# Scaling attention probabilities on GpSimd: a tensor-scalar multiply replaced by a product of two tensors

## The reference, cut to what matters

```python
scores = einsum('bhqd,bhkd->bhqk', Q, K_rep) / 8
scores = scores + polarity_bias + (1 - gtp) * NEG
attn   = softmax(scores, axis=-1)
out    = einsum('bhqk,bhkd->bhqd', attn, V_rep)
```

## Time and profile before

| what | value |
|---|---|
| median of 3 runs | 4389.04 us (4388.15 to 4399.78) |
| span of the profiled execution, first to last instruction | 4385.1 us |
| PE busy | 3923.2 us, 89% |
| DVE busy | 3009.0 us, 69% |
| ACT busy | 2583.3 us, 59% |
| POOL busy | 2416.3 us, 55% |
| mean granted TensorE clock | 0.966 of full speed |
| line L1420 (the scaling), 768 instructions on POOL | 927.1 us busy |

### The profile page before, as it was taken

The page is one execution under the profiler, slowest core; times in us unless marked ns, Lnnn a source line. Parts: engine busy times, 40 slices in busy tenths (PEclk is TensorE's granted clock), DMA queues, the critical chain, the costliest instruction groups (busy, mean ns, idle before and its releaser), DMA issues. The chain is left out here.

```text
span 4385.1 us, 105712 instructions
## 1 busy us (share of the span) xinstructions
PE 3923.2 (89%) x37596; PEld 2574.9 (59%) x37596; DVE 3009.0 (69%) x8821; ACT 2583.3 (59%) x6209; POOL 2416.3 (55%) x3854
## 2 busy tenths in 40 slices
PE   3999999999999999999999999829599999999999
PEld 1565555555556655555555566526366666666666
DVE  4676676676666766766666766562387877788786
ACT  2656556556566565565565665502277777777776
POOL 3657566566475565665664755525455545555452
PEclk7999999999999999999999999959799999999999
DMA  4323334233243233342432432123332433324231
GB/s 126 75 77 84 75 76 92 66 95 85 62 99 73 78 82 77 78 93 65 96 79 68 97 75 77 49 94 60 54 64 45 61 58 54 59 49 70 45 54 26
DMA packets 168566, 317.06 MB, mean 72 GB/s; under 512 B 21680, under 2 KB 112112, under 8 KB 162928
## 3 DMA queue, kind: packets, MB, share of 16 engines
q1 hardware_dynamic: 162928, 300.88, 32.0%
q0 software_dynamic: 3968, 5.25, 0.7%
q10 hardware_dynamic: 1152, 4.19, 0.3%
HBM read 126.66 MB, written 32.59 MB: 36 GB/s over the span
## 5 line engine op out<-in xcount | busy, mean ns | idle before, releaser
L1420 POOL TENSOR_SCALAR l_prob_wo<-l_prob_wo,l_recip_g 128x384 f32<-128x384 f32 (+3 forms) x768 | 927.1, 1219 | 259.5 <-DVE l_recip_g L980 257.6
L1871 DVE TENSOR_REDUCE l_neg_max<-l_bank 128x1 f32<-128x512 f32 x1024 | 680.3, 684 | 260.5 <-PE l_bank L1710 259.9
L1997 ACT ACTIVATE l_pts<-l_bank 128x512 f32<-128x512 f32 x1024 | 593.3, 597 | 296.8 <-PE l_bank L1725 288.1
L1248 ACT ACTIVATE l_prob_wo<-l_prob_wo,l_neg_max_g 128x128 f32<-128x128 f32 (+3 forms) x1024 | 571.0, 559 | 297.9 <-DVE l_neg_max_g L974 291.4
L961 DVE CUSTOM_DVE_ANT_0 l_bank<-l_bank,l_mask 128x128 f32<-128x128 f32 (+3 forms) x1024 | 501.0, 500 | 319.8 <-PE l_bank L648 311.9
L974 DVE CUSTOM_DVE_ANT_0 l_prob_wo<-l_bank,l_bias 128x128 f32<-128x128 f32 (+3 forms) x1024 | 476.1, 483 | 342.5 <-PE l_bank L699 319.6
L1240 ACT ACTIVATE l_pts<-l_bank 128x128 f32<-128x128 f32 (+3 forms) x1024 | 439.3, 437 | 443.2 <-PE l_bank L666 426.8
L710 PE MATMUL l_bank<-ident,l_prob_wo 128*128 128x128 f32 x2560 | 426.5, 283 | 84.0 <-POOL l_prob_wo L1420 38.1
L710 PEld LDWEIGHTS l_bank<-ident,l_prob_wo 128*128 128x128 f32 x2560 | 289.1, 141 | 317.0 <-issue 178.6
L1710 PE MATMUL l_bank<-next_ks,l_qs 96*128 96x512 bf16 x1024 | 393.5, 385 | 46.2 <-DVE l_neg_max L1871 23.1
L1725 PEld LDWEIGHTS l_bank<-l_qs,next_ks 128*128 128x128 bf16 x4096 | 303.5, 97 | 181.1 <-ACT l_pts L1997 30.6
(11 more groups left out here) (262 smaller groups left out, 8081.2 us busy)
## 6 DMA issues: line engine op xcount, KB each, us to landing
l_bias<-bias SPq DMA_DIRECT2D x128, 512.0 KB, 4.4
l_qs<-l_parts SPq DMA_DIRECT2D x192, 128.0 KB
l_qs<-l_qs SPq DMA_DIRECT2D x96, 256.0 KB
l_x<-in_x SPq DMA_DIRECT2D x32, 512.0 KB, 4.7
l_kT<-l_bias SPq DMA_DIRECT2D x128, 128.0 KB, 3.2
l_qT<-l_arena SPq DMA_DIRECT2D x128, 128.0 KB, 3.0
l_qT<-l_bias SPq DMA_DIRECT2D x128, 128.0 KB, 3.0
l_prob_wo<-in_Wo SPq DMA_DIRECT2D x16, 1024.0 KB, 4.8
```

Of the source, the lines that this page charges most:

```text
L1248: nc.scalar.activation(prob[qt][:, i, :], prob[qt][:, i, :], ACT.Exp, bias=neg_max_g[:, k:k + 1], scale=-1.0, accum_out=sums_g[:, k:k + 1] ...
L1420: nc.gpsimd.tensor_scalar(prob[qt][:, i, :], prob[qt][:, i, :], recip_g[:, k:k + 1], None, ALU.mult).then_inc(s.g_scaled, 1)
L1871: nc.vector.tensor_reduce(neg_max[:, n % (2 * UNITS):n % (2 * UNITS) + 1], S[n % SB][:, :], AX.X, ALU.max, negate=True).then_inc(s.max_rea ...
L1997: nc.scalar.activation(pts[:, q % 2, u % H, :, :], TB[u % 2][:, :].rearrange("p (j q) -> p j q", j=NT), ACT.Exp, scale=DS ** -0.5).then_in ...
```

## The change

`scale` multiplied a row by a per-partition scalar: an instruction with one tensor operand and a pointer to a column of 128 numbers. It now multiplies two tensors: the row, and that same column read at step 0, so that each of the row's (qt + 1) * 128 elements meets the same number. Output, semaphores, waits, and the place in POOL's list are the same, and no other instruction of any engine is changed or moved.

```diff
                     k = 2 * p + i
                     pool.wait_ge(s.g_recip, BEATS * b + p + 1)
-                    nc.gpsimd.tensor_scalar(prob[qt][:, i, :], prob[qt][:, i, :], recip_g[:, k:k + 1], None, ALU.mult).then_inc(s.g_scaled, 1)
+                    v = prob[qt][:, i, :]
+                    nc.gpsimd.tensor_tensor(v, v, recip_g[:, k:k + 1].to_broadcast([P, (qt + 1) * P]), ALU.mult).then_inc(s.g_scaled, 1)
```

## The result

The changed kernel took **4402.73 us** (median of 20 runs, 4389.03 to 4414.11), the kernel before 4395.52 (20 runs, 4388.15 to 4404.54): a ratio of 1.0023, 95% interval 1.0015 to 1.0031. That is 7 us slower, inside the 0.3% that was counted as no change, and 35 us above the forecast.

A forecast was written before the change was run, and what follows sets the result against it. PE bounds the kernel, busy 89% of the span; PE waits shortened by 0.69 + 0.41 + 0.23 = 1.33 us in each of 16 sequences save 21 us, giving 4368 us against 4389.04. The 8-in-10 range was 4350 to 4403 us.

The forecast's parts named there:

- the first rival: Slower: POOL's product shuts out DVE's own scaling L984 until it ends, delaying copy and PE; 4415 us, chance 0.17.
- L1081's lead of 0.13 us: Evidence against shut-out: a 256-wide DVE operation starting 0.13 us ahead of a POOL product kept its 0.35 us.
- first sign of being wrong: L984's mean at 256 wide at 0.7 us or more, PE's waits for L993 growing as much as POOL's fall.
- The rival's price: At 256-wide beats, L984 shut out would end at 0.84 instead of 0.35 us, making PE 0.49 us later; 47 us altogether.
- The three places: PE's waits on POOL at 512-wide, 384-wide and a sequence's last row: gains 0.69, 0.41 and 0.23 us, 1.33 a sequence.
- the fourth place: PE's transpose of a 128-wide beat: wait put down to POOL but really for DVE's 512-wide copy; counted as nothing.
- the bound: All PE idle time ending with a scaled row from POOL, about all a faster POOL can give: 38.1 us.
- six places in a sequence: 256-wide beats where shut-out would delay PE by 0.49 us each, over 16 sequences: 47 us.
- The count that the price went by: Eight times in a sequence a 256-wide L984 starts about 0.06 us before POOL's L1420.
- the second rival: No change: other engines close behind give the gain back at the second and third place; 11 us remain, 4378 us, chance 0.22.
- the 17 forecast: PE's waits on POOL fall from 38.1 to about 17 us, what is left being the second and fourth place.
- the change does what it says: Opposing rival: step 0 is read dearly, new instruction no shorter than 1572 ns at 512; 4389 us or more, chance 0.04.

The follow-up runs named there:

- E5: The change plus a one-column POOL memset to an unused tile before each 128- and 256-wide product: 4365.05 us, 0.993 of the kernel before.
- E4: The change, with POOL's 128- and 256-wide products also waiting until DVE's scaling L984 is done: 4363.5 us, 0.993 of the kernel before.
- E2: The change with the new instruction at 384 and 512 wide only, the old one at 128 and 256: 4360.58 us, 0.9931 of the kernel before.
- E9: The change itself, run again beside E7's kernel on one chip: 4404.52 us, 1.002 of the kernel before.
- E10: E7's kernel, run again beside the change on one chip: 4379.15 us, 0.9974 of the kernel before.
- E1: The change with all rows scaled on POOL by the new instruction, DVE's scaling L984 removed: 4362.82 us, 0.9928 of the kernel before.
- E7: The change with DVE's 128-wide scaling moved to POOL, DVE keeping only the 256-wide one: 4379.55 us, 0.9959 of the kernel before.
- E8: The kernel before with all rows scaled on POOL by the old instruction, none on DVE: 4411.89 us, 1.0035 of the kernel before.

## Why the prediction was wrong

**The step that failed** is the weighing of the first rival: "Against it: DVE's start is the earlier one". I took a lead of 0.06 us, read off the start stamps beside the old instruction, and L1081's lead of 0.13 us, which was enough, and gave the rival 0.17. The leads in the change are 0.04 and 0.05 us, and they lose every time; 0.08 us wins every time (E5). L1081's row lay on the far side of that limit and said nothing of the near side. The prediction itself noted that the lead would be smaller; between two outcomes with no row in between, a chance near one half was due. What the runs showed is the rival's mechanism: L984 at 256 wide took 0.81 us in 113 of 128 cases, and PE's waits for L993 rose from 28.8 to 75.5 us, more than those for POOL fell. That is the prediction's own first sign of being wrong.

**What was right.** The instruction: 1044, 828, 621 and 424 ns against estimates of 1049, 835, 622 and 409, and POOL's busy time fell by 331 us (322). The rule of the Trainium skill, "GPSIMD Engine Reference", section "Engine selection" (against VectorE, one-input operations at about line rate, two-input ones about half as fast), isn't borne out where the scalar comes from a column: 1572 ns for the one, 1044 for the product. The rival's price: L984 took 0.81 (0.84), ending 0.15 us behind POOL (0.16). The three places: in the second sequence of the change the waits of 0.69 and 0.23 are gone, and that of 1.10 has shrunk by 0.46 (0.41 forecast):

```profile
426.98 0.55 PE L710 MATMUL l_bank<-ident,l_prob_wo 128*128 128x128 f32 x3 [0.64 <-POOL l_prob_wo L1421]
```

Right, too, was that POOL's wait at the fourth place isn't POOL's: it is 0.44 us in E4, as before.

**What the change alone is worth.** With L984 kept out of the way in E4, it is -26 us in front of L710 and -30 in the median; 21 were forecast, 38 as the bound. Some 5 us of the rest lie in a row that wasn't read: waits for ACT's copies (15.7 to 10.4). The shutting-out then costs 88.2 - 56.5 = 32 us in front of L710, where 0.49 us at six places in a sequence made 47: at the place shown above PE lost 0.42 (0.86 for 0.44), and 32 us over 16 sequences is 2.0 us, or nearly five such places. The count that the price went by was misread as well: L984 at 256 wide starts 0.06 us ahead of L1420 in 82 of 128 cases, five in a sequence and not eight; in the change it is 113, seven in a sequence. The prediction also had no term for the granted clock, by which the two profiles of the change lose 15 and 22 us more than the one of the kernel before.

The 4403 us measured lie at the very edge of the range of 4350 to 4403 us. That is luck: the range left out the worse part of the rival that came true, and it was reckoned from 4389 us, where the kernel before has 4395.5 in 20 runs. The rival's own 4415 us meant 26 us more than before; 7 were measured, since the gain was larger than forecast and the price smaller.

**The other rivals.** The gain was not given back where the second rival had it: the three waits above are shorter or gone, and E4, which leaves those places as the change has them, is 30 us faster. Waits for POOL fell to 9.0 us, below the 17 forecast, because the fourth place now counts as DVE's. And the change does what it says.

## What to carry to other kernels

When an instruction on GpSimd is replaced, look at what VectorE starts at the same moment: a cheaper one can cost more if it keeps VectorE out for its length. If two engines are released by one event and can shut each other out, set their order by a wait (E4) or leave one of them the slower instruction that lets the other through (E2), since start stamps 0.05 us apart don't tell who wins. And read PE's busy time beside its waits: between E9 and E10 it differed by 19 us, the idle time by 7.

## What the runs showed of the hardware that was not expected

- GpSimd's multiplication by a column hardly holds VectorE up: the 256-wide scaling keeps 0.35 us even when the multiplication had started 0.17 to 0.69 us ahead (31 times of 31). The product of two tensors does hold it, to its end (0.81 us). The Trainium skill, "SBUF — State Buffer", section "SBUF: two separate sides", describes an exclusive lock that the first to start holds for its whole instruction. Products that are first agree with that; the multiplication by a column doesn't. With VectorE first, GpSimd is delayed in both forms, 0.61 to 0.74 us for the product (E5) and 0.92 to 1.08 for the multiplication, which is less than what VectorE's record still has to run.
- "First" isn't the start stamp of the record: at 256 wide, POOL's product starting 0.04 to 0.05 us behind DVE's operation got ahead of it 113 times of 113 in the change, and 0.08 to 0.09 us behind it 0 times of 113 in E5.
- The granted clock fell to one half for some microseconds in the middle of the grouped stage in 7 of 14 sequences in both profiles of the change, in 1 to 4 of 14 in E1 to E7 and in none in E8, E10 and the one profile of the kernel before, with the same matmuls in the same order. The cause is open.
